# Start of a four-layer expert kernel: order of routing, ranking and LoRA preparation products, and of one low part

## What is computed

```python
expert = jnp.argmax(cond_8, -1)                       # layer 0: one expert for each batch
x = x + down(silu(up(x)) * gate(x)) + biases          # with that expert's weights, 256 hidden
x = x + x @ W_base.T + b_base + SCALING * sum_e w[b, e] * (x @ As[e].T) @ Bs[e].T
x = x + x @ (sum_g y[b, g] * weight[g] * mask).T + bias
w, sel = top_k(softmax(cond_8), 2)                    # layer 3: two experts of eight and a shared one
x = x + sum_k w[b, k] * mlp(x, expert sel[b, k]) + mlp(x, shared)   # gelu(gate) * up, 512 hidden
```

## Time and profile before

| what | value |
|---|---|
| median of 3 runs | 155.03 us (154.92 to 155.67) |
| profiled execution, its own time | 154.85 us |
| span from first to last instruction | 152.8 us |
| PE busy | 148.2 us |
| DVE busy | 110.3 us |
| POOL busy | 91.5 us |
| ACT busy | 72.1 us |
| moved by DMA | 30.15 MB |

### The profile page before, as it was taken

One profiled execution on the slowest core, in us unless ns is written; L12 is line 12 of the kernel. 1 busy time (PEld: TensorE's weight loads), 2 busy tenths in 40 slices (PEclk: granted clock), 3 DMA queues, 4 the chain that ended last, 5 costly groups with the idle time before them and its releaser, 6 DMA issues.

```text
span 152.8 us, 3109 instructions
## 1 busy us (share of the span) xinstructions
PE 148.2 (97%) x1075; PEld 134.5 (88%) x1075; DVE 110.3 (72%) x229; ACT 72.1 (47%) x138; POOL 91.5 (60%) x93
## 2 busy tenths in 40 slices
PE   7999999999999999999999999999999999999992
PEld 2269999999986999999989999999999999999881
DVE  2886676666896686768876868785587886968772
ACT  2866444452374554544463454545435334346540
POOL 1002999999700005939994949996785999880000
PEclk9999999999999999999999999999999999999999
DMA  3989999994363667294296567086538048000052
GB/s 78 399 264 355 405 410 402 409 416 158 142 231 89 179 163 257 33 311 144 54 324 209 177 236 230 14 263 239 188 101 309 6 116 296 6 0 0 0 207 71
DMA packets 13911, 30.15 MB, mean 197 GB/s; under 512 B 1336, under 2 KB 8008, under 8 KB 13768
## 3 DMA queue, kind: packets, MB, share of 16 engines
q1 hardware_dynamic: 13472, 28.76, 54.5%
q10 hardware_dynamic: 424, 1.20, 2.1%
HBM read 24.71 MB, written 1.05 MB: 169 GB/s over the span
## 4 chain that ended last, share of the span: by engine, by line
PE 86%; DVE 4%; POOL 3%; DMA 2%; ACT 2%; issue 1%; SPq 0%; ACTq 0%; DVEq 0%; POOLq 0%
PE pair L543 22%; PE pair L533 12%; PE acc L592 10%; PE pair L480 9%; PE pair L550 8%; PE acc L577 6%; PE acc L488 5%; PE acc L601 5%; PE pair L447 3%; PE pair L469 2%; PE pair L519 2%; PE pair L512 2%; POOL duo_lo L371 2%; DVE hid L765 2%; DMA lora_sb<-lora 2%; ACT hid_hi L430 2%
## 5 line engine op out<-in xcount | busy, mean ns | idle before, releaser
L371 POOL TENSOR_TENSOR duo_lo<-raw_duo,duo_hi 128x512 fp32r<-128x512 f32 x36 | 48.7, 1352 | 2.9
L756 DVE TENSOR_TENSOR hid_lo<-hid,hid_hi 128x512 fp32r<-128x512 f32 (+1 forms) x41 | 36.5, 892 | 18.0 <-ACT hid_hi L430 17.2
L430 ACT ACTIVATE hid_hi<-hid 128x512 fp32r<-128x512 f32 (+1 forms) x41 | 25.4, 622 | 44.2 <-DVE hid L765 41.2
L368 POOL CAST duo_hi<-raw_duo 128x512 fp32r<-128x512 f32 x36 | 28.4, 788 | 29.1 <-PE acc L592 29.1
L765 DVE TENSOR_TENSOR hid<-pair,act 128x512 f32<-128x512 f32 (+1 forms) x49 | 32.9, 674 | 5.7 <-PE pair L543 4.1
L543 PE MATMUL pair<-x_duo,duo_hi 128*128 128x256 f32 x192 | 35.3, 282 | 0.4 <-issue 0.3
L411 ACT ACTIVATE act<-pair 128x512 f32<-128x512 f32 x48 | 28.4, 591 | 10.1 <-PE pair L543 8.1
L543 PEld LDWEIGHTS pair<-x_duo,duo_hi 128*128 128x128 f32 x192 | 29.6, 188 | 1.4 <-DVE hid L765 0.7
L543 PE MATMUL pair<-x_duo,duo_lo 128*128 128x256 f32 x96 | 26.9, 280 | 0.0
L533 PE MATMUL pair<-x_hl,shared_hi 128*128 128x512 f32 x64 | 20.5, 402 | 0.0
L543 PEld LDWEIGHTS pair<-x_duo,duo_lo 128*128 128x128 f32 x96 | 18.0, 188 | 0.0
(11 more groups left out here) (95 smaller groups left out, 198.1 us busy)
## 6 DMA issues: line engine op xcount, KB each, us to landing
raw_duo<-experts SPq DMA_DIRECT2D x12, 768.0 KB, 5.0
ring<-experts SPq DMA_DIRECT2D x16, 386.5 KB, 6.9
raw_solo<-experts SPq DMA_DIRECT2D x8, 768.0 KB, 5.1
x_duo<-x_hl SPq DMA_DIRECT2D x24, 128.0 KB, 3.5
x<-xT ACTq DMA_DIRECT2D x1, 1024.0 KB, 6.4
lora_raw<-x SPq DMA_DIRECT2D x4, 256.0 KB, 2.4
raw_solo<-shared SPq DMA_DIRECT2D x1, 768.0 KB, 8.9
out<-lora_raw SPq DMA_DIRECT2D x3, 256.0 KB, 2.8
```

The source lines that it names most:

```text
L368: pool.tensor_copy(duo_hi[:, j % HALVES, piece(n)], raw_duo[:, j % RAWS, piece(n)])\
L371: pool.tensor_tensor(duo_lo[:, j % HALVES, piece(n)], raw_duo[:, j % RAWS, piece(n)], duo_hi[:, j % HALVES, piece(n)].bitcast(F32), ALU.su ...
L430: act.activation(hid_hi[:, k % SPLITS, at], hid3[:, u % PAIRS, at], ACT.Copy)\
L756: dve.tensor_tensor(hid_lo[:, k % SPLITS, at], hid3[:, u % PAIRS, at], hid_hi[:, k % SPLITS, at].bitcast(F32), ALU.subtract).then_inc(hid_ ...
```

## The change

Five things change. PE's eight dummies are split: five, then the routing product, then one, then the two ranking products, then two, and all four LoRA products stand behind these; before, the first LoRA product stood ahead of the routing product and three behind the ranking. DVE copies at_row ahead of all four bs_w, no longer between the second and the third. The banks `prep` become three, with acc0 as the third, and the waits on prep_copied count accordingly. In layer 3, low_part(3) stands before hidden_low(0) on DVE.

```diff
--- before.py
+++ after.py
@@ -197,7 +197,7 @@
                 for p in range(PAIRS)]
         acc = [ctx.enter_context(nc.psum_tensor(f"acc{n}", [P, N], F32)) for n in range(2)]
         lin = pair[1] + pair[2]
-        prep = pair[2]
+        prep = pair[2] + acc[:1]
 
         cond_in, rep_in, lora_in = sem("cond_in"), sem("rep_in"), sem("lora_in")
         small_in, w2_in = sem("small_in"), sem("w2_in")
@@ -392,7 +392,7 @@
                 else:
                     k = 2 * (n - G)
                     dst = mix_raw[:, k:k + 2, :, :].rearrange("p k b j -> p (k b j)")
-                act.activation(dst, prep[n % 2][:, :], ACT.Copy).then_inc(prep_copied, 1)
+                act.activation(dst, prep[n % 3][:, :], ACT.Copy).then_inc(prep_copied, 1)
 
             for b in range(B):
                 act.wait_ge(up0_done, b + 1)
@@ -437,27 +437,28 @@
                     pe.matmul(acc[0][:, :].rearrange("p (b n) -> p b n", n=P), zeros[:, :],
                               zeros[:, :].unsqueeze(1).to_broadcast([P, GB, P]), start=True, stop=True)
 
-            pe.wait_ge(zeros_set, 1)
-            warm(8)
-
             def prepare1(q):
                 pe.wait_ge(bsw_done, q + 1)
-                if q >= 2:
-                    pe.wait_ge(prep_copied, q - 1)
-                pe.matmul(prep[q % 2][:, :], lora_sb[:, AS1:AS1 + P],
+                if q >= len(prep):
+                    pe.wait_ge(prep_copied, q - len(prep) + 1)
+                pe.matmul(prep[q % 3][:, :], lora_sb[:, AS1:AS1 + P],
                           bs_w[:, q * GB:(q + 1) * GB, :].rearrange("p b o -> p (b o)"),
                           start=True, stop=True).then_inc(prep_mm, 1)
 
-            prepare1(0)
+
+            pe.wait_ge(zeros_set, 1)
+            warm(5)
             pe.wait_ge(ones_set, 3)
             pe.wait_ge(at_diag_done, 1)
             pe.matmul(acc[1][:, 0:B], ones_b[:, :], at_diag[:, :], start=True, stop=True).then_inc(at_mm, 1)
+            warm(1)
 
             pe.wait_ge(chosen_done, 1)
             pe.matmul(pair[1][0][0:B, 0:E], earlier_b[:, :], chosen_b[:, :], start=True, stop=True)
             pe.matmul(pair[1][0][0:B, E:2 * E], ones_b[:, 0:B], chosen_b[:, :], start=True, stop=True)\
               .then_inc(rank_mm, 1)
-            for q in range(1, G):
+            warm(2)
+            for q in range(G):
                 prepare1(q)
 
             pe.wait_ge(ydelta_done, 1)
@@ -465,8 +466,8 @@
             for k in range(E):
                 n = G + k // 2
                 if k % 2 == 0:
-                    pe.wait_ge(prep_copied, n - 1)
-                ins = pe.matmul(prep[n % 2][:, (k % 2) * B * R:(k % 2 + 1) * B * R], w2_sb[:, k, :],
+                    pe.wait_ge(prep_copied, n - len(prep) + 1)
+                ins = pe.matmul(prep[n % 3][:, (k % 2) * B * R:(k % 2 + 1) * B * R], w2_sb[:, k, :],
                                 y_delta[:, :, :].rearrange("p b j -> p (b j)"), start=True, stop=True)
                 if k % 2 == 1:
                     ins.then_inc(prep_mm, 1)
@@ -637,11 +638,10 @@
                                       cond_sb[:, IOTA:IOTA + E].unsqueeze(1).to_broadcast([B, K, E]), ALU.is_equal))
             dve.tensor_tensor(chosen_b[:, :], onehot[:, 0, :], onehot[:, 1, :], ALU.add).then_inc(chosen_done, 1)
             dve.wait_ge(rep_in, 16)
+            dve.wait_ge(at_mm, 1)
+            dve.tensor_copy(at_row[:, :], acc[1][0:1, 0:B]).then_inc(at_done, 1)
             dve.wait_ge(lora_in, 16)
             for q in range(G):
-                if q == 2:
-                    dve.wait_ge(at_mm, 1)
-                    dve.tensor_copy(at_row[:, :], acc[1][0:1, 0:B]).then_inc(at_done, 1)
                 at = slice(q * GB, (q + 1) * GB)
                 dve.scalar_tensor_tensor(
                     bs_w[:, at, :], lora_sb[:, BS1:BS1 + P].unsqueeze(1).to_broadcast([P, GB, P]), LORA_SCALE,
@@ -792,8 +792,8 @@
 
             product(0)
             low_part(2)
+            low_part(3)
             hidden_low(0)
-            low_part(3)
             product(1)
             hidden_low(1)
             for u in range(2, UNITS + 2):
```

## The result

| | before | changed |
|---|---|---|
| median (runs) | 155.10 us (7) | 153.82 us (7) |
| lowest to highest | 154.65 to 155.67 | 153.45 to 154.62 |
| ratio, 95% interval | | 0.9914, 0.9893 to 0.9935 |
| profiled execution, its own time | 154.85 us | 153.57 us |
| span | 152.8 us | 151.6 us |

The change made the kernel 1.28 us faster, in the medians and in the two profiled executions alike; forecast were 153.9 us and a gain of 1.1. A second set of 7 runs gave 154.06 us, ratio 0.9931 (0.9905 to 0.9957).

What follows compares the result with a forecast made beforehand. PE, busy 97% of the span, was taken as the bound, so only its own losses could be won. Start 0.6 plus hand-over 0.5 gave 1.1 us: 155.03 - 1.1 = 153.9 us, range 153.4 to 154.9.

Steps and rivals of the forecast that it cites:

- Start: From the first dummies to the slot product L497: it would start at 12.67, a gain of 0.6 us, ends 0.4 and 0.75.
- the ends 11.47 and 11.77: Better and cautious times for PE to reach the first expert product, which stood at 12.29 before.
- the step that made the payload the limit: At the start, DVE's payload, ending at 12.58, was taken to limit the slot product and the 0.6 us gain.
- small_sb's landing of 4.6 us: At the start, small_sb issued at 2.02 would land at 6.62, so y_delta starts at 6.66, 0.43 us earlier.
- the payload's bound of 12.64: At the start, the earliest time the payload allows the slot product: 12.58 + 0.06.
- The early copy: At_row's copy at the start: first expert load issued at 4.35, worth nothing by itself, necessary once L480 starts earlier.
- Hand-over: Into the last layer: low part and gather 0.79 us earlier, first pair group ends 0.60 earlier; 0.5 taken, ends 0.65 and -0.1.
- The new wait at down(0): At the hand-over, hidden_low(0) ends at 46.19, so down(0) on PE may wait up to 0.1 us.
- new waits: Sign of being wrong: down products waiting for low parts behind 50 us, which would give the second gain back.
- A: Only one of the two places, start or hand-over, pays: 154.5 us; chance 0.24.
- C: At the start, x or small_sb lands late beside the ring loads: 155.6 us at worst, 154.2 for small_sb; chance 0.07.
- B: At the start, PE's clock rises 3.5 us later, losing 1.75 us: 155.6, or 156.2 if the second place fails; chance 0.07.

Runs made afterwards that it cites:

- after_again: The changed kernel once more, nothing altered: 154.06 us.
- front_only: The changed kernel with low_part(3) again behind hidden_low(0): 154.53 us, ratio 0.9957 to the kernel before.
- before_banks: The kernel before with the third preparation bank alone: 154.80 us, ratio 0.9981 to the kernel before.
- two_banks: The changed kernel with two preparation banks instead of three: 154.39 us.
- copy_late: The changed kernel with the copy of at_row behind all four bs_w on DVE: 154.26 us.
- low_only: The kernel before with only low_part(3) moved ahead of hidden_low(0): 154.54 us, ratio 0.9960 to the kernel before.
- dummies_first: The changed kernel with all eight dummies ahead of the routing product again: 156.53 us, ratio 1.0082 to the kernel before.
- three_less: The changed kernel with five dummies only, none behind the routing product: 155.35 us.

## Why the prediction was right

**Start, 0.6 us forecast, 0.66 measured in one pair of profiles.** PE's order did what the sum said: L481 at 11.63, between the ends 11.47 and 11.77. Part of the 0.66 is luck of the clock. The first pair of passes took 1.13 us before, against 0.86 at the full rate, so its rise came near 4.53 + 2 x 0.27 = 5.07, not at the end of the dummies at 4.42 as the prediction read it; in the changed kernel's profile it came near 4.7. With a rise as late as before's, the last two dummies would have taken 0.97 us, as in after_again, and L481 would be 0.17 us later: an estimate of 0.49 us for the order alone, beside the 0.54 of front_only's medians. The routing product, the copy and the first load came within 0.1 us of the worked-out times (3.22, 3.45, 4.35 against 3.26, 3.56, 4.44). What failed is the step that made the payload the limit. It read the payload as what L497 waited for before, but L497 followed L480 at the same 0.98 us as in the changed kernel, with the payload ready 0.26 us earlier and no wait in the profile: PE's own order was the limit already. And it took small_sb's landing of 4.6 us from one profile as fixed. Of the 13 profiles of this study two show 4.5 or 4.6 and the others 3.7 to 4.0; y_delta starts at 6.12, right behind bs_w, and the payload was 0.54 us earlier than predicted. PE, not the payload, set the slot product. The number came out because the payload's bound of 12.64 lay between the two ends of PE's, 12.45 and 12.75: that is luck. That the payload can be the bound is shown by before_banks, where PE waits for it at 13.05.

**The parts of the start.** The third bank is worth 0.40 us in two_banks' profile and 0.21 alone, where the payload caps it. The early copy is worth nothing at the first load, as forecast, and is needed, as forecast, but for the thirteenth load: by 0.58 us in copy_late's profile. The split of the dummies is what makes the early copy affordable; without it DVE's bs_w waits, and PE loses its clock besides.

**Hand-over, 0.5 us taken, 0.60 worked out and measured.** The first gather left SP 0.66 us before down(0) (45.05 against 45.71), where it was 0.14 behind it (46.50 against 46.36): 0.80 earlier, 0.79 forecast. The new wait at down(0), 0.12 us, was put at up to 0.1. That PE had waited for the gather was argued before. low_only and front_only show that the order of the two DVE operations decides it: the idle went with the new order and came back with the old one. The exchange also moves DVE's later products, and the trace of before names one of them at the pair product:

```profile
48.27 0.68 DVE L765 TENSOR_TENSOR hid<-pair,act 128x512 f32<-128x512 f32 x1
49.61 0.30 PEld L543 LDWEIGHTS pair<-x_duo,duo_hi 128*128 128x128 f32 x2 [0.68 <-DVE hid L765]
```

That product had ended at 48.95, 0.66 us before, so the wait was for something else. The gather remains: the weight load follows SP's first gather issue by 3.11 us in before (46.50 to 49.61) and in front_only (47.11 to 50.22). No row names it.

**No loss behind.** Where the prediction feared new waits, the last short stall near the end is still there and 1.28 us earlier:

```profile
119.52 0.13 issue
119.65 1.64 PE pair L544 x12
```

against 120.93 in the chain before. The full 1.2 us of span arrive at the end.

**Rivals.** A (half a gain) is excluded by front_only and low_only together: each is faster than before, beyond its interval. C did not occur: x landed at 2.41 + 6.1, and no profile shows PE waiting for it. B, the late clock, did not decide the change, but it is real: in the two pairs of profiles of one program it accounts for the difference of the spans, and in dummies_first and three_less it decides the result. That it makes the spread of all kernels' runs is likely, not shown. I had given it the price of 1.75 us for 3.5 us of delay. In three_less, with a rise about 3.3 us later, the LoRA products take 5.44 us (4.37 to 9.81 in the chain) instead of 3.43 (4.91 to 8.34), 2.0 more; as they begin 0.54 earlier, L481 is 1.47 late. What I had not seen is that before is subject to it as much as the changed kernel, as low_only's profile shows (8 unbroken dummies, yet two passes of 1.96 us instead of 1.13). The Trainium skill ("TensorE: Matmul & The Clock Gate", Part 1) says that the moment of the rise varies from run to run; the profiles here agree, with rises from about 4.6 to 7 us.

## What to carry to other kernels

A product that starts a long chain (here expert numbers, loads) can be put among warm-up products instead of behind them, if the warm-up goes on around it: the same eight dummies cost nothing more, while the two kernels with a pause of 0.8 us ahead of the LoRA products were 1.3 to 1.5 and 2.5 to 2.7 us slower. When the first issue of a queue moves, look at the later transfers in it too: in copy_late it was not the first load that PE waited for but the thirteenth. And a landing time read from one profile is a sample: where a term hangs on it, keep both bounds.

## What was not expected of the hardware

The rise of PE's clock moved between executions of one program: L481 began at 11.79 and 12.27, spans 151.6 and 152.1. In the kernels without a long pause it lay between about 4.6 and 7 us from the start, and with 0.80 us of idle of PE in the first 5.7 us near 7.9 and 10. The granted clock of the profiles reads 1.00 in all of this (0 to 5 and 5 to 8 us, all thirteen profiles); the pitch of the weight loads, 0.85 against 0.43 us, shows the level.
